# Attention of layer 0: probabilities and values as high and low parts, three single-pass products in place of one in full precision

## The reference

```python
def _L0_attn_ref(x, Wq, bq, Wk, bk, Wv, bv, Wo, bo):
    ...
    q = (x @ Wq + bq).reshape(b, h, t, dh)
    k = (x @ Wk + bk).reshape(b, t, h, dh).transpose(0, 2, 3, 1)
    v = (x @ Wv + bv).reshape(b, t, h, dh).transpose(0, 2, 1, 3)
    logits = jnp.einsum('bhtd,bhds->bhts', q, k) * scale
    mask = jnp.triu(jnp.full((t, t), -jnp.inf, dtype=x.dtype), k=1)
    weights = jax.nn.softmax(logits + mask, axis=-1)
    out = jnp.einsum('bhts,bhsd->bhtd', weights, v)
    out = out.transpose(0, 2, 1, 3).reshape(b, t, h * dh)
    return out @ Wo + bo
```

## Time and profile before

| | us |
|---|---|
| median of 3 runs | 1678.1 (1677.97 to 1679.89) |
| the profiled execution | 1685.7 |
| its span | 1683.7 |
| TensorE busy in it | 1532.6 (91%) |
| VectorE busy | 1014.5 (60%) |
| ScalarE busy | 674.0 (40%) |
| GpSimd busy | 341.6 (20%) |

### The profile page before, as it was taken

How to read it: one execution, slowest core, us unless ns; L and a number is a source line. 1 busy time by engine, 2 the same in 40 slices (tenths; PEclk the granted TensorE clock), 3 DMA queues, 4 the chain that set the end, 5 groups by cost and what they waited for, 6 DMA issues and landing times. The chain is left out here.

```text
span 1683.7 us, 20881 instructions
## 1 busy us (share of the span) xinstructions
PE 1532.6 (91%) x7643; PEld 1080.8 (64%) x7643; DVE 1014.5 (60%) x1911; ACT 674.0 (40%) x1300; POOL 341.6 (20%) x250
## 2 busy tenths in 40 slices
PE   7999999999999658998996899899698999989998
PEld 5788888877767423576885355455584555556887
DVE  6777777712323689346445789898345777744444
ACT  1355555501121230301322599896251555533221
POOL 3100000001303100104005069497641000000000
PEclk9999999999899779989998989899899999999999
DMA  5200000042322300014552013121001343101212
GB/s 185 72 14 19 13 19 13 7 125 67 118 75 67 115 1 0 1 50 139 193 179 65 27 63 100 50 101 63 16 1 23 74 104 91 23 1 46 62 58 63
DMA packets 93905, 105.26 MB, mean 63 GB/s; under 512 B 13909, under 2 KB 77513, under 8 KB 93694
## 3 DMA queue, kind: packets, MB, share of 16 engines
q1 hardware_dynamic: 90750, 95.86, 19.0%
q0 software_dynamic: 3072, 8.30, 1.6%
HBM read 83.39 MB, written 14.55 MB: 58 GB/s over the span
## 5 line engine op out<-in xcount | busy, mean ns | idle before, releaser
L989 POOL TENSOR_TENSOR m_state_c<-m_state,m_c 128x1024 f32<-128x1024 f32 x64 | 153.4, 2399 | 86.9 <-DVE m_state L2870 71.2
L2870 DVE TENSOR_TENSOR_SCAN m_state<-m_decay,psum 128x512 f32<-128x512 f32 x128 | 148.9, 1207 | 14.2 <-POOL m_state_c L989 9.4
L3018 DVE TENSOR_REDUCE a_max_pieces<-psum 128x4 f32<-128x512 f32 (+2 forms) x176 | 107.8, 639 | 51.7 <-PE psum L1740 29.8
L2227 ACT ACTIVATE a_probT<-psum 128x512 f32<-128x512 f32 (+1 forms) x176 | 97.3, 558 | 89.4 <-PE psum L1767 85.9
L1608 PE MATMUL psum<-m_state_c,ident 128*128 128x512 f32 x256 | 121.0, 596 | 3.8 <-POOL m_state_c L989 3.8
L936 POOL TENSOR_TENSOR rstd<-var_eps,half_neg 128x4 f32<-128x4 f32 x18 | 20.4, 1131 | 431.5 <-DVE var_eps L2313 431.3
L2578 DVE TENSOR_TENSOR f_h<-f_silu,psum 128x512 f32<-128x512 f32 (+1 forms) x46 | 31.4, 685 | 108.1 <-ACT f_silu L1981 94.4
L1088 PE MATMUL psum<-ones_bf,ident_bf 128*128 128x512 bf16 x311 | 80.4, 416 | 16.8 <-ACT m_t L2059 4.6
L1981 ACT ACTIVATE f_silu<-psum 128x512 f32<-128x512 f32 (+1 forms) x46 | 27.5, 597 | 166.5 <-PE psum L1271 132.5
L2158 ACT ACTIVATE m_b_inputT<-m_dtuT,m_bcT 128x256 f32<-128x256 f32 x218 | 93.1, 496 | 0.7 <-PE psum L1600 0.6
L1600 PEld LDWEIGHTS psum<-ident,m_b_inputT 128*128 128x128 f32 x512 | 62.0, 151 | 42.8 <-DVE m_state L2870 35.3
(11 more groups left out here) (457 smaller groups left out, 3539.8 us busy)
## 6 DMA issues: line engine op xcount, KB each, us to landing
f_fc<-in_L_ffn_fc_w_dram SPq DMA_DIRECT2D x16, 1024.0 KB, 5.8
m_c<-m_c_rows SPq DMA_DIRECT2D x32, 512.0 KB, 3.6
f_share<-f_share_rows SPq DMA_DIRECT2D x32, 256.0 KB, 3.3
f_out_rows<-f_out SPq DMA_DIRECT2D x15, 256.0 KB, 2.2
f_slot_rows<-f_out SPq DMA_DIRECT2D x1, 2560.0 KB, 9.6
f_rows_in<-f_slot_rows SPq DMA_DIRECT2D x10, 256.0 KB, 3.0
wkv<-in_L_attn_Wk_dram SPq DMA_DIRECT2D x16, 128.0 KB, 2.2
wkv<-in_L_attn_Wv_dram SPq DMA_DIRECT2D x16, 128.0 KB, 2.2
```

Of the source, the lines that this page charges most:

```text
L989: pool.tensor_tensor(hc2[c][:], h2[c][:], c_wide[v][:].rearrange("p (b s) -> p b s", b=BATCH), ALU.mult).then_inc(s_hc, 1)
L2227: act.activation(probT3[n % 2][:, PROB3[i]:PROB3[i] + wide], bank[TURNED3[at % 3]][:, 0:wide], ACT.Exp).then_inc(s_exp3, 1)
L2870: ins = dve.tensor_tensor_scan(h2[c][:, b], dec2[c][:, b], bank[4 + 2 * c + b], 0.0, ALU.mult, ALU.add)
L3018: dve.tensor_reduce(max_of3[n % 2][:, int(diagonal), t_, heads[0]:heads[-1] + 1], o, AX.X, ALU.max).then_inc(s_max3, 1)
```

## The change

Values and transposed probabilities each get a high and a low tile of type F32R, and `attend` forms three single-pass products for key tiles 0 to 2. The last key tile (128 columns) stays one product in float32, on copies of its own (`v_last0`, `pT_last0`). ScalarE now makes all high parts and both `last` copies, VectorE all low parts, by subtraction from PSUM. `s_pT0` and `s_pT1` count two steps a unit, where they counted one. The next unit's value product waits for the first maximum of this unit (`s_nmax`), which stands behind the value subtraction on VectorE. The renumbering of a semaphore shared with a later stage is left out.

```diff
@@ -150,14 +150,16 @@
         q_low0 = wo_.take("a0_q_low", [DH0, SEQ], F32R)
         k_low0 = wo_.take("a0_k_low", [DH0, SEQ], F32R)
         q_first0, k_first0 = (wo_.take(f"a0_{c}_first", [DH0, P]) for c in "qk")
-        v0 = w.take("v0", [P, BATCH, ST, DH0])
+        v_high0, v_low0 = (w.take(f"a0_v_{c}", [P, BATCH, ST, DH0], F32R) for c in ("high", "low"))
+        v_last0 = w.take("a0_v_last", [P, BATCH, DH0])
 
 
         CAUSAL = ST * (ST + 1) // 2 * P
         T_AT = {3: 0, 2: 512, 0: 896, 1: 1024}
         S_AT = {0: 0, 1: 512, 3: 896, 2: 1024}
         prob = w.take("prob", [P, CAUSAL])
-        probT = w.take("probT", [P, CAUSAL])
+        pT_high0, pT_low0 = (w.take(f"a0_probT_{c}", [P, CAUSAL], F32R) for c in ("high", "low"))
+        pT_last0 = w.take("a0_probT_last", [P, P])
         wq_next0 = [prob[:, u * KT * DH0:(u + 1) * KT * DH0].rearrange("p (k d) -> p k d", k=KT) for u in range(2)]
         nmax = w.take("nmax", [P, ST])
         rsum = w.take("rsum", [P, ST])
@@ -1125,7 +1128,8 @@
                     pe.wait_ge(s_wkv0[u], 32 * i + 32)
                     pe.wait_ge(s_wl, SPLIT_Q0 + 2 * i + u + 1)
                 split_product(bank[1][:], u, b).then_inc(s_k_mm, 1)
-                pe.wait_ge(s_v, n)
+                if not early(n, 1):
+                    pe.wait_ge(s_nmax, 3 * n - 2)
                 for j in range(ST):
                     for k in range(KT):
                         s0 = b * SEQ + j * P
@@ -1138,7 +1142,7 @@
                 pe.wait_ge(s_k, n + 1)
                 for j in (3, 2, 0, 1):
                     if j == 1 and not early(n, 1):
-                        pe.wait_ge(s_pT1, n)
+                        pe.wait_ge(s_pT1, 2 * n)
                     o = bank[3 + T_AT[j] // 512][:, T_AT[j] % 512:T_AT[j] % 512 + (j + 1) * P]
                     if j == 0:
                         pe.matmul(o, q_first0[:], k_first0[:], start=True, stop=False)
@@ -1169,16 +1173,17 @@
             def attend(n, b):
 
                 pe.wait_ge(s_v, n + 1)
+                pe.wait_ge(s_nmax, 3 * n + 1)
                 if not early(n, 1):
                     pe.wait_ge(s_o, n)
-                for i in range(ST):
-                    if i == 0:
-                        pe.wait_ge(s_pT0, n + 1)
-                    if i == 1:
-                        pe.wait_ge(s_pT1, n + 1)
-                    mm = pe.matmul(bank[6][:, i * P:], v0[:, b, i, :], probT[:, S_AT[i]:S_AT[i] + (ST - i) * P],
-                                   start=(i == 0), stop=(i == ST - 1))
-                mm.then_inc(s_o_mm, 1)
+                for i in range(ST - 1):
+                    if i < 2:
+                        pe.wait_ge(s_pT1, 2 * n + i + 1)
+                    o, cols = bank[6][:, i * P:], slice(S_AT[i], S_AT[i] + (ST - i) * P)
+                    pe.matmul(o, v_high0[:, b, i, :], pT_high0[:, cols], start=(i == 0), stop=False)
+                    pe.matmul(o, v_high0[:, b, i, :], pT_low0[:, cols], start=False, stop=False)
+                    pe.matmul(o, v_low0[:, b, i, :], pT_high0[:, cols], start=False, stop=False)
+                pe.matmul(bank[6][:, (ST - 1) * P:], v_last0[:, b, :], pT_last0[:], start=False, stop=True).then_inc(s_o_mm, 1)
 
             pe.wait_ge(s_xT0, 2)
             pe.wait_ge(s_xT1, 2)
@@ -1947,7 +1952,8 @@
                     for b in range(BATCH):
                         n = 4 * i + 2 * u + b
                         act.wait_ge(s_v_mm, n + 1)
-                        act.copy(v0[:, b], bank[2][:].rearrange("p (j d) -> p j d", j=ST)).then_inc(s_v, 1)
+                        act.copy(v_last0[:, b], bank[2][:, (ST - 1) * P:])
+                        act.copy(v_high0[:, b], bank[2][:].rearrange("p (j d) -> p j d", j=ST)).then_inc(s_v, 1)
                         for r, j in enumerate((3, 2, 0, 1)):
                             if j != 0:
                                 act.wait_ge(s_nmax, 3 * n + min(r, 2) + 1)
@@ -1957,7 +1963,11 @@
                         if not (last and u == 1 and b == 1):
                             keys_high(2 * i + (2 * u + b + 1) // 2, n + 1, (b + 1) % 2)
                         act.wait_ge(s_pT_mm, 3 * n + 1)
-                        act.copy(probT[:, 0:512], bank[0][:]).then_inc(s_pT0, 1)
+                        act.copy(pT_high0[:, 0:512], bank[0][:]).then_inc(s_pT0, 1)
+                        act.wait_ge(s_pT_mm, 3 * n + 3)
+                        act.copy(pT_high0[:, 512:1024], bank[7][:])
+                        act.copy(pT_high0[:, 1024:1280], bank[5][:, 256:])
+                        act.copy(pT_last0[:], bank[7][:, 384:512]).then_inc(s_pT0, 1)
                     if not last:
                         split_key(i + 1, u)
 
@@ -2374,6 +2384,8 @@
                 for u in range(2):
                     for b in range(BATCH):
                         n = 4 * i + 2 * u + b
+                        dve.wait_ge(s_v, n + 1)
+                        dve.tensor_tensor(v_low0[:, b], bank[2][:].rearrange("p (j d) -> p j d", j=ST), v_high0[:, b].bitcast(F32), ALU.subtract)
                         for r, j in enumerate((3, 2, 0, 1)):
                             if j != 0:
                                 dve.wait_ge(s_sc, 3 * n + min(r, 2) + 1)
@@ -2392,9 +2404,12 @@
                             keys(2 * i + (2 * u + b + 1) // 2, n + 1, (b + 1) % 2)
                         if not early(n, 1):
                             output(2 * i + (2 * u + b + 1) // 2 - 1, n - 1, 1 - b)
-                        dve.wait_ge(s_pT_mm, 3 * n + 3)
-                        dve.tensor_copy(probT[:, 512:1024], bank[7][:])
-                        dve.tensor_copy(probT[:, 1024:1280], bank[5][:, 256:]).then_inc(s_pT1, 1)
+                        dve.wait_ge(s_pT0, 2 * n + 1)
+                        dve.tensor_tensor(pT_low0[:, 0:512], bank[0][:], pT_high0[:, 0:512].bitcast(F32), ALU.subtract).then_inc(s_pT1, 1)
+                        dve.wait_ge(s_pT0, 2 * n + 2)
+                        dve.tensor_tensor(pT_low0[:, 512:1024], bank[7][:], pT_high0[:, 512:1024].bitcast(F32), ALU.subtract)
+                        dve.tensor_tensor(pT_low0[:, 1024:1280], bank[5][:, 256:], pT_high0[:, 1024:1280].bitcast(F32),
+                                          ALU.subtract).then_inc(s_pT1, 1)
 
 
             with dve.Fori(0, HEADS0 // 2) as i:
```

More of the change, by code:

```diff
@@ L182, in build @@
         s_pT_mm = sem("a0_prob_turned_or_f1_last_expert_spread")
-        s_pT0, s_pT1 = sem("a0_probT_s0_or_f1_last_weights_ready"), sem("a0_probT_rest_ready")
+        s_pT0, s_pT1 = sem("a0_probT_high_or_f1_last_weights_ready"), sem("a0_probT_low_ready")
         s_o_mm = sem("a0_pv_product_or_f1_last_weights_turned")
@@ L395, in build @@
         ONE_HOT_1, TURNED_1, SPREAD_1 = HEADS0 * BATCH, HEADS0 * BATCH, 3 * HEADS0 * BATCH
+        COPIED_1 = 2 * HEADS0 * BATCH
         w, wo_ = work.fresh(), w_odd.fresh()
@@ L1504, in turn_last_weights @@
                     else:
-                        pe.wait_ge(s_pT0, TURNED_1 + c)
+                        pe.wait_ge(s_pT0, COPIED_1 + c)
                     for h in range(CT):
@@ L1512, in spread_last @@
                 def spread_last():
-                    pe.wait_ge(s_pT0, TURNED_1 + 4)
+                    pe.wait_ge(s_pT0, COPIED_1 + 4)
                     pe.wait_ge(s_eo, SLOTS_1 + EXPERTS1)
```

## The result

The changed kernel took 1690.7 us at the median (1690.0 to 1694.2, 4 runs) against 1678.2 before: a ratio of 1.0076 (95% interval 1.0059 to 1.0094), **12.5 us slower**, where 12.3 was forecast. Repeated on the chip of the first experiments it gave 1689.0 against 1678.2, 1.0057 (1.0043 to 1.0071), 10.8 us slower. The ratios are estimated from the runs of both kernels together with their interval; they are not the ratios of the medians and differ from them by up to 0.2%, as the runs of the kernel before lie in two groups, near 1677 and 1682 us.

The account below looks back on a forecast made before the run. TensorE's own spacing was taken as the bound. Unit 1 -0.35, units 2 to 30 +10.4, last unit +1.4 and last product +0.8 made +12.3 on 1678.1, so 1690.4 us; range 1683 to 1701.

Parts of the forecast that it names:

- The place: TensorE ahead of each unit's 256-column j=1 scores: a gap of about 0.6 us, waiting for VectorE's low parts.
- The relay: ScalarE copies, then VectorE subtractions, release the j=1 scores at T + 2.10 us; T ends a unit's last transpose.
- The small copies: ScalarE's copies of 256 and 128 columns out of PSUM, priced at 371 and 264 ns.
- The product: Probabilities times values on TensorE: 2.16 us becomes 1.81 with a 0.08 saving at its end, 0.35 saved a unit.
- the first product's extra 0.10 after a stall: TensorE's first j=1 score product after the wait costs 0.10 us more, its weights not loaded ahead.
- The ends: First and last units of the stage: unit 1 -0.35 us, last unit +1.4, last product +0.8.
- VectorE's cycle: Rival: VectorE becomes the bound, its cycle 8.8 to 9.0 us against TensorE's 9.05; 1695 to 1700 us, chance 0.14.
- The clock: Rival: TensorE's idle gaps lower the granted clock in one unit in eight; +33 us, 1723, chance 0.03.
- passes it on whole: The output product after the stage starts on the last result and carries the full +12.3 us onward.

Follow-up runs that it names:

- the first experiments: The changed kernel again, and three edits of it (longer ScalarE copy, bank 5 copied first, value subtraction later), on one chip; unedited 1689.0 us against 1678.2.
- v_low_late: Changed kernel with the value subtraction moved behind the four maxima on VectorE: 1695.8 us, ratio 1.0095 to the kernel before.
- both_moved: Changed kernel with bank 5's columns copied ahead of bank 7's and the value subtraction behind the maxima: 1685.0 us, ratio 1.0040 to the kernel before.
- after_filled: Changed kernel with TensorE's idle time at the end of the stage filled by unused products: 1685.0 us, ratio 1.0034 to the kernel before.
- full_product: Changed kernel with one full-precision product on the high tiles, low parts made but unused: 1704.9 us, ratio 1.0146 to the kernel before.
- one_product: Changed kernel with only high by high multiplied, the other two products left out: 1679.2 us, ratio 1.0006 to the kernel before.
- values_last: Changed kernel, bank 5 copied first, value subtraction behind the maxima, next value product behind probabilities times values: 1667.5 us, ratio 0.9930 to the kernel before.
- relay_wide: Changed kernel with ScalarE's last copy of transposed probabilities widened from 128 to 384 columns: 1694.4 us, ratio 1.0101 to the kernel before.

## Why the prediction was right

- **The place.** The idle time stands where it was put, ahead of the 256-column scores, in each unit, due to the low parts. By starts it is 0.61 us, as forecast (2.15 - 1.54); the profile's own row says 0.42, as it counts from the end of the mask record.
- **The relay.** T + 2.10 was forecast and T + 2.13 measured (TensorE at T + 2.19 against 2.15). The small copies were 6 and 19 ns above their prices; VectorE took 0.61 from start to start and 0.41 for its last part, forecast 0.60 and 0.42.
- **The product.** 1.89 forecast, 1.88 measured; values 1.70 and 1.70; keys 1.47 and 1.47.
- **The mis-sized term** is the first product's extra 0.10 after a stall, with its weights not loaded ahead. The j=1 scores took 0.50 (158.07 to 158.57) against 0.48: 0.02. The 0.10 does occur elsewhere: where v_low_late and both_moved stall the value product, its 16 records take 2.05 against 1.95. Why it is absent at the scores is not shown. So a unit became 9.00, not 9.05, and the loss 0.31, not 0.36; over 29 units 1.5 us.
- **The ends.** Unit 1: 9.31 to 8.97, -0.34 (forecast -0.35). Last unit: 6.94 to 8.38 filled, +1.4 (+1.4). Last product: 2.72 to 3.59 filled, +0.9 (+0.8). With the units, 29 x 0.306 = 8.9, that is **+10.9 by the mechanism**.
- **VectorE's cycle.** 8.8 to 9.0 was forecast, 8.73 measured, 0.27 below the change's unit. The near tie was real: removing the stall alone gained that much and no more.
- **The pages.** By the Trainium skill, VectorE: DVE Perf Modes, "The TRN2 errata", the small copies were estimated at 357 and 250 ns; the trace has 377 and 283, so the price worked out from rows was the nearer. The Trainium skill, VectorE: DVE Perf Modes, "The DRAIN you can't avoid", says that the next operation does not start until the pipeline is empty, and adds that one that is not held starts earlier; here a subtraction of 0.69 was followed after 0.61 (156.99 to 157.60), as the rows before had it.
- **The clock** was given 0.03, as falls within units. None came there. But one came behind the last unit, where TensorE is idle for 2.3 us in place of the 1.2 of the earlier trace rows, and cost 3.2 us (0.1 + 1.0 + 2.1), which the sum did not have. The forecast said of the output product that it "passes it on whole"; it did not, it took 2.1 longer to its first result.
- **The total** is right partly by offsetting. The stage, clock included, is 14.1 us longer by the traces, and the medians rose by 12.5 and 10.8. If the stage took as long in the runs without a profile, the rest of the program, whose code is the same, gave back 1.6 to 3.3 us, and that the +12.3 was hit so closely is in part luck. The same holds beyond this kernel: in ten of the eleven traces with the change in it the stage has grown by 1.6 to 5.2 us more, or shrunk by that much less, than the medians say (3.8 in after_filled); full_product alone goes the other way, by 5.6. Which stage gives it back, and why, stays open.

## What to carry to other kernels

When a product is split to save TensorE time, price the release of its buffers first: count from the last write of the buffer to the point at which TensorE wants it back, with every copy that must precede in series. The cheaper product saved its 0.35 us a unit even with the wait in place, but the wait cost 0.66. The order of the copies (the bank that is wanted first, first) was worth 0.27, until VectorE's chain was the next bound; and the whole gain came only when the value product no longer waited either. Look at the end of a loop as well as within it: there the new dependence cost 2.3 us by itself and 3.2 by the clock, and filling TensorE's idle time gave the 3.2 back in the trace.

## What the runs showed of the hardware

The granted clock fell to half, 1.2 GHz, at the end of this stage in all nine traces of the change and its unfilled variants, and in none of the filled ones nor in the kernel before. Ahead of the last transposes TensorE was idle for 1.75 us (v_low_late) to 3.41 us (one_product) in the nine, 2.34 with the change, and for 1.19 in the kernel before. With the change the granted clock was 0.50 from about 353 to 363 us. Idle times of 0.4 to 0.6 us in each unit never lowered it. In three of the nine the fall was over before the output product mattered (16.43 us to its first result, as before); in values_last it cost 3.5 us there (19.94).

The remainder of the program, from the last addition of the output product to the end of the span, runs the same code in all thirteen traces and took between 1259.5 us (relay_wide) and 1274.1 us (the kernel before), 1265.0 with the change. The falls of the clock lie at other places in each. That is why single profiled executions were compared by stage only, and why medians that differ by a few us were not read as effects.
